# The low parts of five weight pieces made on GpSimd during the front, in place of VectorE

## The reference

```python
def _L0_xattn_ref(q, k, v, mask, gamma, beta):
    logits = jnp.einsum('bsd,btd->bst', q, k) / jnp.sqrt(d_k)
    logits = jnp.where(mask == 0, NEG, logits)
    x = jnp.einsum('bst,btd->bsd', jax.nn.softmax(logits, axis=-1), v)
    xhat = (x - mu) * jax.lax.rsqrt(var + EPS)
    return xhat * gamma + beta

def _L0_ffn_ref(x, w_gate, w_gate_up, w_down):      # 8 experts, K = 2, F = 1024
    gate_probs = softmax(x @ w_gate)                # top 2 kept and rescaled to sum 1
    g, u = jnp.split(jnp.einsum('bsd,edh->ebsh', x, w_gate_up), 2, axis=-1)
    expert_out = jnp.einsum('ebsf,efd->ebsd', jax.nn.silu(g) * u, w_down)
    return jnp.einsum('bse,ebsd->bsd', gate_probs, expert_out)

x = x + _L0_xattn_ref(_layernorm(x), ctx, ctx, mask, gamma, beta)
x = x + _L0_ffn_ref(_layernorm(x), w_gate, w_gate_up, w_down)
```

## Time and profile before

| | |
|---|---|
| median of 3 runs | 446.84 us (446.77 to 446.87) |
| the profiled execution, own time | 448.5 us |
| its span, first to last instruction | 446.6 us |
| TensorE / VectorE / ScalarE / GpSimd busy | 425.7 / 305.7 / 216.4 / 193.3 us |
| mean granted clock of TensorE | 0.986 |

### The profile page before, as it was taken

The page is one execution under the profiler, slowest core; times in us unless marked ns, Lnnn a source line. Parts: engine busy times, 40 slices in busy tenths (PEclk is TensorE's granted clock), DMA queues, the critical chain, the costliest instruction groups (busy, mean ns, idle before and its releaser), DMA issues.

```text
span 446.6 us, 10141 instructions
## 1 busy us (share of the span) xinstructions
PE 425.7 (95%) x2356; PEld 351.7 (79%) x2356; DVE 305.7 (68%) x757; ACT 216.4 (48%) x461; POOL 193.3 (43%) x207
## 2 busy tenths in 40 slices
PE   9899889899999999999999999999999999999990
PEld 5797457688888888888888888888888888888880
DVE  4678978776787478767866567768865678746540
ACT  4686726354554366365533455545634456333330
POOL 5463122544464334644544443446633347543221
PEclk9999999899999999999999999999999999999995
DMA  7785423553455235524631225424541144211121
GB/s 209 200 252 179 175 72 112 119 174 72 99 141 128 38 72 133 151 36 122 175 73 25 30 37 153 137 72 120 129 131 25 24 112 84 42 28 24 13 26 12
DMA packets 28621, 44.17 MB, mean 99 GB/s; under 512 B 2833, under 2 KB 22219, under 8 KB 28587
## 3 DMA queue, kind: packets, MB, share of 16 engines
q1 hardware_dynamic: 20358, 32.96, 24.4%
q0 software_dynamic: 7520, 10.41, 14.3%
q10 hardware_dynamic: 709, 0.32, 0.3%
HBM read 34.04 MB, written 9.65 MB: 98 GB/s over the span
## 4 chain that ended last, share of the span: by engine, by line
PE 86%; DVE 6%; issue 2%; POOL 1%; DMA 1%; DVEq 1%; ACT 1%; POOLq 0%
PE bank L1428 45%; PE bank L1451 15%; PE bank L1453 8%; PE bank L1441 7%; PE bank L1226 2%; PE bank L1412 2%; PE bank L1272 1%; PE bank L1305 1%; PE bank L1295 1%; DMA tok<-rows_d,gather_i 1%; PE bank L1258 1%; PE bank L1498 1%; DVE x_sb L674 1%; DVE token_sel L725 1%; POOL row_rstd L578 0%
## 5 line engine op out<-in xcount | busy, mean ns | idle before, releaser
L1428 PE MATMUL bank<-w,tokT_hi 128*128 (+1 forms) x616 | 171.2, 400 | 1.6 <-DVE tokT_lo L892 0.9
L1146 ACT ACTIVATE gated<-bank,row_rstd 128x512 f32<-128x512 f32 x77 | 52.9, 687 | 177.0 <-PE bank L1428 152.9
L1428 PEld LDWEIGHTS bank<-w,tokT_hi 128*128 128x128 f32 x616 | 110.9, 190 | 23.9 <-issue 1.4
L1451 PE MATMUL bank<-w,aT_hi 128*128 (+1 forms) x304 | 116.4, 417 | 0.0
L901 DVE SCALAR_TENSOR_TENSOR act<-bank,row_rstd,gated 128x512 f32<-128x512 f32 x77 | 57.6, 748 | 78.9 <-ACT gated L1146 78.9
L585 POOL DMA_INDIRECT out<-y_sb,out_i x39 | 61.9, 1588 | 83.8 <-DVE y_sb L922 79.7
L1428 PE MATMUL bank<-w,tokT_lo 128*128 (+1 forms) x308 | 95.8, 392 | 0.0
L1453 PE MATMUL bank<-w,aT_lo 128*128 (+1 forms) x304 | 85.3, 281 | 0.0
L572 POOL TENSOR_TENSOR tok<-tok,beta_b 128x256 f32<-128x256 f32 x36 | 26.2, 729 | 102.6 <-DMA tok<-rows_d,gather_i 102.6
L1428 PEld LDWEIGHTS bank<-w,tokT_lo 128*128 128x128 f32 x308 | 58.1, 189 | 13.0
L1451 PEld LDWEIGHTS bank<-w,aT_hi 128*128 128x128 f32 x304 | 57.2, 188 | 10.7 <-issue 0.2
(11 more groups left out here) (188 smaller groups left out, 409.3 us busy)
## 6 DMA issues: line engine op xcount, KB each, us to landing
raw<-in_L_ffn_w_gate_up SPq DMA_DIRECT2D x32, 512.0 KB
raw<-in_L_ffn_w_down SPq DMA_DIRECT2D x16, 512.0 KB
rows_d<-x_sb SPq DMA_DIRECT2D x8, 265.0 KB
x_sb<-in_x SPq DMA_DIRECT2D x8, 256.0 KB, 8.1
out<-x_sb SPq DMA_DIRECT2D x8, 256.0 KB
out<-y_sb,out_i POOLq DMA_INDIRECT x39
tok<-rows_d,gather_i POOLq DMA_INDIRECT x38, 3.7
cap<-in_mask_BxSxS_ik SPq DMA_DIRECT2D x1, 462.0 KB, 7.3
```

What stands on the lines that cost most here:

```text
L1146: act_e.activation(gated[:, h, :], ps_g[h][:, :], ACT.Silu, scale=row_rstd[:, s:s + 1]).then_inc(gated_set, 1)
L1428: ins = pe.matmul(ps[:, :], tokens_[:, s, k, :], w.rearrange("p a g d -> p (a g) d"), start=(k == 0 and tokens_ is tokT_hi and part == 0), ...
L1451: pe.matmul(ps_y[:, :], aT_hi[:, h, c, :], w.rearrange("p a t d -> p (a t d)"), start=(h == 0 and c == 0), stop=False, skip_group_check=True)
```

## The change

GpSimd makes the low parts of pieces 0 to 4, one in each of its iterations i = 4 to 8, behind the att_scale of batch i - 1 and in front of the gamma product of batch i + 1. VectorE makes only piece 5, in its old place, and waits for w_lo to reach 5 first, so that the count stays in order. ScalarE makes the high part of piece 4 directly behind its loop, in front of the `numbers` of groups 0 and 1 (copies of the comparison tables scaled by the token's number, on which the token matmuls wait) rather than behind them. `split_low` itself is the same function, called with the other engine.

```diff
--- before.py
+++ after.py
@@ -553,6 +553,8 @@
                     x_rstd(i + 2)
                 if i >= 1:
                     scales(i - 1)
+                if i >= 4:
+                    split_low(pool, i - 4)
                 if i + 1 < B:
                     values_gamma(i + 1)
 
@@ -830,10 +832,6 @@
             for i in range(B + 1):
                 if i + 2 < len(STATS):
                     x_stats(i + 2)
-                if i == 3:
-                    split_low(dve, 0)
-                if i == 4:
-                    split_low(dve, 1)
                 if i + 1 < B:
                     masked_logits(i + 1)
                 if i == 0:
@@ -846,7 +844,6 @@
                     choose(GROUPS[0])
                 if i == 5:
                     slots(0, GROUPS[0])
-                    split_low(dve, 2)
                 if i == 6:
                     places(0, GROUPS[0])
                     select(0, GROUPS[0])
@@ -969,7 +966,6 @@
 
             tok_low(0, 0)
             row_gate(0, 0, 0)
-            split_low(dve, 3)
 
             after(tables)
             step(tables, dve.tensor_scalar(expert_i[:], expert_t[:], 1, None, ALU.bitwise_and))
@@ -982,11 +978,11 @@
             row_centre(1, 1)
             gate_half(0, 0, 0)
             row_stats(1, 1)
-            split_low(dve, 4)
             tok_low(1, 1)
             row_gate(1, 1, expert_of(1))
             gate_half(0, 0, 1)
             act_low(0, 0)
+            dve.wait_ge(w_lo, PIECES - 1)
             split_low(dve, PIECES - 1)
             row_centre(2, 0)
             dve.wait_ge(expert_places, 1)
@@ -1122,9 +1118,9 @@
                     split_high(act_e, i - 2)
                 if i == 6:
                     split_high(act_e, 3)
+            split_high(act_e, 4)
             numbers(0, GROUPS[0])
             numbers(1, GROUPS[1])
-            split_high(act_e, 4)
             act_e.activation(silu_ready[:], neg_half[:, 0:1], ACT.Silu)
             split_high(act_e, 5)
```

## The result

The changed kernel takes 455.51 us (median of 4 runs, 453.65 to 456.48) against 446.8 us before in the same series. The ratio is 1.0201 (95% interval 1.0183 to 1.0219), about 9.0 us slower by the ratio (8.7 between the two medians). I had forecast slower, 452.3 us. The kind of mechanism was right (GpSimd's splits hold up VectorE), but not the list of what they hold; the loss is 1.6 times what I gave, and the time lies just above my range, which ended at 455.5.

The account below looks back on a forecast made before the run. VectorE's chain from 41 to 86 us was taken to move the end, TensorE bounding the rest. Holds +5.0, clock +1.0 and third gather -0.5 gave +5.5, 452.3 us on the median; range 447.5 to 455.5.

Parts of the forecast that it names:

- The length of a split: GpSimd's two-input instruction of 1,024 columns: 2.45 us, from 2.0 to 2.9, against 1.22 on VectorE.
- The ports: GpSimd reading SBUF holds up VectorE instructions with two SBUF inputs for the whole instruction; reads of PSUM are not held.
- The step that failed: Which VectorE instructions GpSimd's splits hold: two-input ones, such as neg_max of batches 5 (1.7 us later) and 6 (2.7 later).
- the clock's cost behind the loop: TensorE's gaps in 45 to 54 us lower its clock at the token matmuls: 0 to 1.6 us, taken as +1.0.
- more than one such stretch: Sign of being wrong: TensorE's loss of clock in the front is larger than one stretch.
- case A: neg_max of batch 7 goes before GpSimd's split 2: places at 42.85 (+1.0), the last choice +4.4.
- case B: GpSimd's split 2 goes before neg_max of batch 7: places at 45.0 (+3.15), the last choice at 53.9 (+5.6).
- The third gather: Without VectorE's split 4 the power before it shortens: 0.9 us earlier, of which 0.5 reaches block 3 (-0.5).
- The 1.6 us of the prediction: Lost before the change by twelve expert matmuls at 1.2 GHz after TensorE's 1.99 us gap: 4.33 us against 2.75.
- Held in part: Rival: ports change hands inside a long GpSimd instruction, VectorE loses tenths each time; +1 to +3, 449 us, chance 0.10.
- Not held: Rival: VectorE goes first and GpSimd waits, no clock change; 446.3 us, no change that can be told, chance 0.09.
- Faster by the clock before block 3: Rival: VectorE not held, and a shorter wait before block 3 keeps TensorE at 2.4 GHz; -2.1, 444.7 us, chance 0.09.

Follow-up runs that it names:

- e10: A kernel by itself, no layer computed: GpSimd subtractions of 128x1024, each beside one VectorE instruction of another form; held ones took 2.02 to 2.16 us.
- e11: The changed kernel with GpSimd's splits 1 and 3 waiting until the experts of the group are chosen: 452.07 us, ratio 1.0115.
- e1: The kernel before with only ScalarE's part of the change, the high part of piece 4 in front of the numbers: 446.48 us, ratio 1.0001.
- e12: The kernel before with the loads of pieces 3, 4 and 5 two batches later in SP's queue, no GpSimd split: 446.62 us, ratio 0.9999.
- e8: The kernel before with eight spin matmuls where TensorE waits for the tokens of block 3: 446.69 us, ratio 0.9990.
- e3: The changed kernel with ten spin matmuls of TensorE in front of the ranks of the first group: 452.75 us, ratio 1.0143.

## Why the prediction was right in kind and wrong in size

**The length of a split**: 2.45 us forecast, 2.35 measured. The estimate from the Trainium skill ("GPSIMD Engine Reference", elementwise cycle accounting) was 2.3 and nearer.

**The ports**: VectorE's instruction is held to the end of the 2.35 us, in the changed kernel and in e10, and not only for a part of them. The Trainium skill ("SBUF — State Buffer", the two sides of SBUF) has it so, and the traces agree (neg_max and split 0 end at 33.72 and 33.70).

**The step that failed** is the list of what is held. I wrote that GpSimd holds up "a VectorE instruction with two SBUF inputs", and passed over `chosen`, a tensor_scalar from SBUF to SBUF (e10 shows that it is held, e11 that sparing it gives 3.8 us back). It was not the timing that misled me: by the forecast's own times `chosen` was due at 37.1 (35.38 and the 1.7 us of the first hold), inside a split 1 from 37.0 to 39.45. I gave the hold to the neg_max of batch 6, which has 2.6 us of slack and in the change took 0.31 us. In the trace split 1 began at 36.10 and met `chosen` at 36.20, for which TensorE's ranks wait, with 0.3 us of slack left. The Trainium skill ("SBUF — State Buffer", the two sides of SBUF) names such a case beside the one with two inputs, a VectorE instruction in a two-port mode; I had looked only for rows of the two-input kind. No trace here shows the mode of `chosen`, only that it is held.

**What followed from it.** TensorE idled 1.9 us and fell to 1.2 GHz, and its matmuls between 39 and 44.6 us, on which x1 and places wait, were slow. I had put the clock's cost behind the loop, at the token matmuls, +1.0. There is a second stretch at the lower clock there (0.83 in 55 to 65), but it costs little: from the last choice to the first gather it takes 8.79 us (63.89 - 55.10), 8.36 before. I had named more than one such stretch as a sign of being wrong. I had also said that up to 41 us slack would absorb the holds. In the profile places began at 45.0 against 41.77, and the front of this execution ran 0.8 us early (neg_max of batch 5 at 31.66 against 32.43; e1, with the front of before, has it at 31.65), so the delay is 4.0 us; case A had 1.0 and case B 3.15.

**From places to the last choice**: 10.1 us against 6.6, +3.5 (chosen 2.1, slot subtraction 1.5). Case A had 3.4 to 3.5, from other instructions, so this agreement is luck (and its terms add up to 3.55). The sum to the last choice was +4.4 to +5.6 and measured +6.8, or +7.5 with the early start.

**The third gather**: forecast 0.9 earlier and 0.5 of it reaching block 3. In GpSimd's timeline it comes 10.9 us behind the first, 12.0 before:

```profile
63.89 0.96 POOL L566 DMA_INDIRECT tok<-rows_d,gather  x1 [8.74 <-DVE gather L870]
...
74.78 1.01 POOL L566 DMA_INDIRECT tok<-rows_d,gather_i  x1 [0.18 <-PE bank L1408]
```

The turn of block 3 comes 28.3 us behind the first gather, 29.1 before: 0.9 gained. TensorE's wait before it is 1.97 us all the same (1.99 before, I had said 1.5), as its own work in front of it moved too.

**The profile against the runs.** First gather +7.2 us, block 3 -0.9, and -1.3 because the matmuls behind it took 3.04 us in this execution, at full clock, where they took 4.33 in the earlier trace rows, at the lower one:

```profile
92.60 1.39 PE bank L1424 x6
94.10 1.65 PE bank L1424 x6
```

That is 5.0 of the 5.2 us. That the two profiles differ by 5.2 us, close to my +5.5, is therefore luck. The profiled execution before had lost 1.3 us to the clock at block 3, and took 448.5 us, 1.7 above the median. Those of e1 and e12, behind the same wait, had not lost it: the twelve matmuls take 1.39 and 1.65 or 1.66 us there as well. (The 1.6 us of the prediction were counted from 2.75 us, the time of later twelves, and so were 0.3 too many.) The profiled execution of the change is 1.9 below its median. With these two the 5.2 us become the 8.7 between the medians. Against the profile of e12 (span 445.0), whose clock does not fall at block 3, the change is 6.8 us longer. The other three runs of the change have a lower mean clock (0.973, 0.972, 0.968 against 0.978) and spans of 453.3, 454.0 and 454.6 us, 1.5 to 2.8 longer. That goes with the clock, but no trace of them was kept, and where in them it falls is open.

**The rivals.** Held in part: out. Not held: out. Faster by the clock before block 3: out, and e8 shows that there was at most 0.9 us to gain there.

**Costed at nothing**: ScalarE's order (e1) and the loads (e12) were rightly so.

## What to carry to other kernels

Before a long two-input instruction goes to GpSimd, list every VectorE instruction that can fall into its time, one-input ones from SBUF to SBUF too, and ask of each who waits for it. Put the GpSimd work behind an instruction for which TensorE waits, not beside it (3.8 us of 9 here), or where VectorE reads PSUM and reduces. A hold that leaves TensorE idle can be paid twice, as time and as clock (the spins of e3 gave 2.6 us back). And look for the cheap half of such a change first: moving one VectorE split into a wait of VectorE gained 0.36%, without the second engine.

## What the runs showed of the hardware that I had not expected

A tensor_scalar of 48 columns, float32 to bf16 or bf16 to bf16, and one of 47 columns, wait 2 us for a GpSimd instruction that reads SBUF; one of a single column (0.14 us) does not. One VectorE instruction can last through four GpSimd instructions in a row (3.11 us). TensorE's clock did or did not fall after the same 2 us of waiting: 4.33 us for twelve matmuls in one execution, full clock in two others (e1, e12).
